# Mixture-of-experts layer: one region of rows per expert for the whole input instead of one per batch, and outputs put together block by block

## What is computed

```
x = x + attention(layernorm(x), ctx, ctx, mask) @ W_out.T
z = layernorm(x)
q = tanh(z @ proj_w.T / 0.3);  logits = -(6 - q @ anchors.T) / 2 / temp
top 2 of 6 experts, softmax of their logits -> expert_weights
h = gelu(z @ w1[e]);  x + sum over the 2 experts e of weight[e] * (h @ w2[e])
```

## Time and profile before

| | before |
|---|---|
| three runs, median (range) | 720.03 us (714.55 to 720.48) |
| the profiled execution | 721.91 us, its span in the trace 720.2 us |
| PE busy | 617.0 us (86%) |
| DVE busy | 451.5 us (63%) |
| ACT busy | 341.8 us (47%) |
| POOL busy | 301.0 us (42%) |
| moved by DMA | 126.25 MB, mean 175 GB/s |
| chain that ended last | PE 55%, DVE 14%, issue 11%, DMA 7%, POOL 5% |

### The profile page before, as it was taken

One profiled execution on the slowest core, in us unless ns is written; L12 is line 12 of the kernel. 1 busy time (PEld: TensorE's weight loads), 2 busy tenths in 40 slices (PEclk: granted clock), 3 DMA queues, 4 the chain that ended last, 5 costly groups with the idle time before them and its releaser, 6 DMA issues.

```text
span 720.2 us, 15169 instructions
## 1 busy us (share of the span) xinstructions
PE 617.0 (86%) x4628; PEld 467.8 (65%) x4629; DVE 451.5 (63%) x968; ACT 341.8 (47%) x646; POOL 301.0 (42%) x434
## 2 busy tenths in 40 slices
PE   5989999999999999988788999999999999996000
PEld 4765566666656656444568898998999888885000
DVE  4846756665685866444986555684555676666455
ACT  4536855666847655574844554433333333331000
POOL 5423755555456656557671314130002233222774
PEclk9759999999999999899987999999999999999555
DMA  5301213222212373347372656485787788886787
GB/s 187 93 30 46 88 63 101 76 87 75 88 59 101 108 271 129 133 172 263 132 263 88 208 174 239 149 273 203 263 293 244 256 268 285 295 277 220 226 246 243
DMA packets 62577, 126.25 MB, mean 175 GB/s; under 512 B 7974, under 2 KB 11046, under 8 KB 62508
## 3 DMA queue, kind: packets, MB, share of 16 engines
q1 hardware_dynamic: 52268, 91.80, 37.7%
q0 software_dynamic: 10240, 33.56, 14.5%
HBM read 69.24 MB, written 56.10 MB: 174 GB/s over the span
## 4 chain that ended last, share of the span: by engine, by line
PE 55%; DVE 14%; issue 11%; DMA 7%; POOL 5%; SPq 3%; ACT 2%; DVEq 1%; POOLq 0%; ACTq 0%
PE ps L1477 7%; DMA y_d<-ysb 5%; PE ps L1499 4%; PE ps L1635 4%; PE ps L1522 3%; PE ps L1687 3%; PE ps L1524 3%; PE ps L1688 3%; PE ps L1523 3%; PE ps L1689 3%; PE ps L1711 3%; PE ps L1713 3%; PE ps L1673 3%; PE ps L1712 3%; PE ps L1590 3%
## 5 line engine op out<-in xcount | busy, mean ns | idle before, releaser
L802 POOL DMA_INDIRECT yg<-y_d,sidx x64 | 64.1, 1002 | 170.4 <-DVE wst L1320 133.9
L1078 DVE TENSOR_REDUCE nmax<-ps 128x4 f32<-128x512 f32 x128 | 82.3, 686 | 45.6 <-PE ps L1477 45.4
L917 ACT ACTIVATE prob<-ps 128x512 f32<-128x512 f32 x128 | 66.1, 603 | 84.2 <-PE ps L1502 81.4
L729 POOL DMA_INDIRECT xs_d<-x,place_now x64 | 67.2, 1049 | 81.0 <-PE ps L1689 66.8
L1687 PE MATMUL ps<-w1H,xgH 128*128 x296 | 90.5, 306 | 2.9 <-DVE xgL L1344 2.9
L1688 PE MATMUL ps<-w1H,xgL 128*128 x296 | 83.9, 283 | 0.0
L1689 PE MATMUL ps<-w1L,xgH 128*128 x296 | 83.8, 283 | 0.0
L996 ACT ACTIVATE xgH<-ps 128x512 fp32r<-128x512 f32 x74 | 44.2, 597 | 80.9 <-PE ps L1673 68.7
L1477 PEld LDWEIGHTS ps<-kfT,qT 32*128 32x128 f32 x1024 | 69.6, 202 | 18.9 <-issue 16.3
L1477 PE MATMUL ps<-kfT,qT 32*128 32x128 f32 x1024 | 76.9, 295 | 1.9 <-DVE nmax L1078 1.4
L1357 DVE COPY ysb<-ps 128x512 f32<-128x512 f32 x74 | 51.0, 689 | 31.4 <-PE ps L1713 19.6
(11 more groups left out here) (195 smaller groups left out, 1373.2 us busy)
## 6 DMA issues: line engine op xcount, KB each, us to landing
xg<-xs_d SPq DMA_DIRECT2D x74, 256.0 KB
y_d<-ysb SPq DMA_DIRECT2D x74, 256.0 KB
xin<-in_x SPq DMA_DIRECT2D x32, 256.0 KB, 2.7
x<-in_x SPq DMA_DIRECT2D x32, 256.0 KB
x_d<-x SPq DMA_DIRECT2D x32, 256.0 KB
x2t<-x_d SPq DMA_DIRECT2D x16, 256.0 KB, 4.1
x2c<-x_d SPq DMA_DIRECT2D x16, 256.0 KB, 4.7
out_x<-x2c SPq DMA_DIRECT2D x16, 256.0 KB
```

Of the source, the lines that this page charges most:

```text
L729: nc.gpsimd.indirect_dma_start(xs_d, bass.IndirectOffsetOnAxis(ap=place_now[:, n % 2, k, t:t + 1], axis=0), x2[:, n % 4, t, :], None).then ...
L802: nc.gpsimd.indirect_dma_start(yg[:, k, z, :], None, y_d[b], bass.IndirectOffsetOnAxis(ap=sidx[:, k, z:z + 1], axis=0))\
L917: nc.scalar.activation(prob[v % 2][:, h, :], ps[:, B_SC + h, :], ACT.Exp, scale=scale).then_inc(exp_done, 1)
L1078: nc.vector.tensor_reduce(nmax[:, n % 2, :, g * hpg + h], ps[:, token_bank(v, h), :].rearrange("p (t k) -> p t k", t=4), axis=AX.X, op=ALU ...
```

## The change

1. **One region for each expert** over both batches: `region` is 4096 + 128 rows. Only 6 tiles can be part filled in all, so `tiles` is (8192 + 6 x 127) // 128 = 69.
2. **Two lists of tiles.** The first `T1` = 32 - 5 = 27 tiles are full tiles of what the first four blocks (`NB1`) left; the other `T2` = 42 are ordered by the block whose rows complete them. So the tiles that hold the rows of blocks 0 to n are among the first `TILES_OF[n]`: 37 for n up to 3, then 45, 53, 61, 69. The new functions are `full_tiles`, `first_list`, `tiles_of_classes`, `first_of_classes`, `list_of` and `rows_to_tiles`. A list comes out with one tile in a partition (`lst`); PE turns it into a row (`turn_list`) and DVE keeps it (`keep_list`). `turn_list` for the first list is in the last step but one of attention, for the second in slot 23. `rows_of_tokens` runs for one block in a slot, slots 24 to 31.
3. **The router's blocks come every 7 slots** instead of 8, and one of the four transposes of a block (`t == 2`) moves to the slot's end.
4. **Padding once**: `fill_up` is called once, in slot 21, instead of once for each batch.
5. **Puts**: put c belongs to slot 46 + 4c // 3 (three in four slots), for all 32 in turn. Its gathers are issued two slots earlier (POOL also waits there for `up_ready`), its store two slots later, and the residual of put c + 16 is loaded five slots later; the first 16 residuals are loaded in slots 28 to 43. 23 puts have a slot in the loop, 9 come behind it. There are six buffers for gathered rows (`RY`), 16 for residuals (`RX`). The gathers read their row numbers straight from `y_row`, and `stage` is gone.
6. **The copy to `ysb`** is ACT's from tile 26 (`BY_ACT`) on.
7. **Everything is written out**: 19 iterations, 76 slots, where there were 20 iterations and 80 slots with hardware loops in them.

The core of the diff:

```diff
-    NT = (2 * seq + EXPERTS * (P - 1)) // P
-    tiles = batches * NT
+    NB1 = blk_per_batch
+    region = batches * seq + P
+    def most_tiles(n):
+        return (2 * n * blk + EXPERTS * (P - 1)) // P
+    T1 = 2 * NB1 * blk // P - (EXPERTS - 1)
+    tiles = most_tiles(nblk)
+    TILES_OF = [most_tiles(max(n + 1, NB1)) for n in range(nblk)]
+    RY, RX, RD = 6, 16, 4
...
-        SPAN = 8
+        SPAN = 7
-        TABLE = SPAN * LATE - 1
+        TABLE = SPAN * (LATE - 1) + 5
...
+        ONE_Y, BY_ACT = 20, 26
+        def put_slot(c):
+            s = TILES_OF[0] + 9 + 4 * c // 3
+            return s if s < SLOTS and TILES_OF[c // 4] < tiles else None
...
+                    for c in puts(TPI * i + k - 2):
+                        store_out(c)
+                    for c in puts(TPI * i + k - 5):
+                        if c + RX < ntok:
+                            load_residual(c + RX)
...
+            def fetch_outputs(c):
+                pool.wait_ge(yrow_done, c // 4 + 1)
+                after(pool, cmb_done, c - RY + 1)
                 for z in range(2):
+                    nc.gpsimd.indirect_dma_start(yg[:, c % RY, z, :], None, y_d[0:TILES_OF[c // 4] * P, :],
...
+                    for c in puts(TPI * i + k + 2):
+                        pool.wait_ge(zp_ready, nblk)
+                        pool.wait_ge(up_ready, min(TPI * i + k - L_UP + 1, tiles))
+                        landed(c)
+                        fetch_outputs(c)
...
+                    w, p, n = tl(i, k, L_DN)
+                    if live(w, tiles) and w >= BY_ACT:
+                        act.wait_ge(y_ready, w + 1)
+                        after(act, y_out[p], 16 * n)
+                        nc.scalar.activation(ysb[:, p, :], ps[:, y_bank(w, p), :], ACT.Copy).then_inc(ya_done, 1)
...
+            def turn_list(bank, count):
+                pe.wait_ge(lst_done, count)
+                for z in range(2):
+                    last = nc.tensor.transpose(ps[0:1, bank, z * P:(z + 1) * P], lst[:, z:z + 1], ident[:])
+                last.then_inc(lst_turned, 1)
...
+            pe.wait_ge(tab_done, 2)
             for t in range(4):
                 project(INSIDE, t)
-            pe.wait_ge(tab_done, 3)
...
+                    if TPI * i + k == TABLE + 4:
+                        pe.wait_ge(used_done, nblk)
+                        turn_list(B_LATE, 2)
```

More of the change, by code:

```diff
@@ L80, in xattn_moe @@
     x2_d = dram("x2_d", [nblk, 4, P, emb], F32)
-    xs_d = dram("xs_d", [batches * rows, emb], F32)
+    xs_d = dram("xs_d", [rows, emb], F32)
     x2_rows = x2_d.rearrange("n t p d -> (n t) p d")
-    y_d = [dram(f"y{b}_d", [NT * P, emb], F32) for b in range(batches)]
+    y_d = dram("y_d", [tiles * P, emb], F32)
     ctx = ExitStack()
@@ L652, in _ @@
+            expert_loop(experts)
+            left = [c for c in range(ntok) if put_slot(c) is None or put_slot(c) + 2 >= SLOTS]
+            for c in left:
+                store_out(c)
+            for c in range(RD):
+                sp.wait_ge(o_out[c], 16 * (ntok // RD))
         @block.gpsimd
@@ L1292, in attention @@
                 if (i, q) == (blk_per_batch + 2, 0):
-                    tiles_of_experts(0)
+                    full_tiles()
                 if (i, q) == (blk_per_batch + 2, 1):
-                    experts_of_tiles(0)
-                if (i, q) == (blk_per_batch + 2, 2):
-                    rows_of_tiles(0)
-                    table(0)
+                    first_list()
                 if (i, q) == (blk_per_batch + 2, 3):
-                    rows_of_tokens(0)
+                    keep_list(B_SC, 0, T1)
                 setup(s)
@@ L1353, in experts @@
                     w, p, n = tl(i, k, L_DN)
-                    if live(w, tiles):
+                    if live(w, tiles) and w < BY_ACT:
                         dve.wait_ge(y_ready, w + 1)
@@ new lines, in experts @@
+                    if TPI * i + k == TABLE + 2:
+                        first_of_classes()
+                    if TPI * i + k == TABLE + 3:
+                        list_of(CLASSES, nblk)
+                        dve.wait_ge(share_done, nblk)
+                    if TPI * i + k == TABLE + 4:
+                        keep_list(B_LATE, T1, T2)
+                        rows_to_tiles()
+                    rows_of_tokens(TPI * i + k - TABLE - 5)
+                    for c in puts(TPI * i + k):
+                        put_together(c)
@@ L1403, in _ @@
+            expert_loop(experts)
+            for c in range(ntok):
+                if put_slot(c) is None:
+                    put_together(c)
         @block.tensor
```

516 lines of the change are left out of this document (238 added, 278 removed).

## The result

The changed kernel takes 676.98 us (median of four runs, 674.82 to 682.66); the kernel before, on the same chip, 719.83 us (714.55 to 720.48). The ratio is 0.943, with a 95% interval of 0.936 to 0.949. The forecast was 687, with a range of 670 to 708. Direction and range held; the kernel came out 10 us faster than the number.

A forecast was written before the change was run, and what follows sets the result against it. PE was taken to bound the loop, with transfers sharing from slot 50, then a tail of POOL's gathers. 567.3 (slot 50's copy) + 68 (dense) + 20.4 (last six slots) + 31.3 (tail) = 687.0 us; range 670 to 708.

The forecast's parts named there:

- PE's pace to slot 50: Expert loop up to slot 50: a slot is PE's work, 3.47 us each.
- signs of being wrong: Wrong if slots 51 to 67 stay at 3.5 us or pass 4.7, or the loop before slot 50 loses over 6.
- the first rival: Slots 51 to 67 stay at PE's pace, 59 us, with a tail of 27.7: 672 us in all; chance 0.17.
- The tail: Behind the last copy: 22 gathers issued one by one by POOL, 1.42 us apart, 31.3 us instead of 56.8.
- The dense slots: Slots 51 to 67: 83 transfers, 21.8 MB, paced by the DMA engines, 68 us, 4.0 a slot.
- a full share is 331 to 336 GB/s: DMA ceiling for slots 51 to 67, from 288 GB/s at share 0.87 and 272 at 0.81.
- The last six slots: Six slots from slot 67 to the last copy in slot 73: 20.4 us, as the last six took before.
- The list: Head of slot 23: PE waits 3.4 us for the second list, plus 2.0 us for the lower clock.
- The router's 8.8 us: Slots 5 to 20: the router's work is the same, so its 8.8 us stay, in 7 slots a block.
- The padding: Moves from slots 32 and 33 to slot 21 at equal price.
- The end of attention: Ahead of the expert loop: the list `used` comes 1.8 us earlier but PE waits for `keep_list`, net +0.6 us.

The follow-up runs named there:

- again2: The changed kernel, unchanged, repeated a second time: 678.46 us, 0.943 of the kernel before.
- half_puts: Changed kernel with put c at slot 46 + 2c, so 15 puts in the loop and 17 behind it: 696.72 us, 0.970.
- full_puts: Changed kernel with one put in every slot from slot 46 on, 28 in the loop and 4 behind it: 680.81 us, 0.942.
- extra1: Changed kernel with one extra 256 KB store of zeros in each of slots 51 to 67: 686.82 us.
- again: The changed kernel, unchanged, repeated for a second profile: 678.57 us, 0.945 of the kernel before.
- spread_fill: Changed kernel with the six padding transfers issued one per slot in slots 20 to 25, not all in slot 21: 678.92 us.
- extra2: Changed kernel with two extra 262,144-byte stores of zeros in each of slots 51 to 67: 702.54 us.
- fill_late: Changed kernel with all six padding transfers issued in slot 24 instead of slot 21: 690.62 us.
- late_turn: Changed kernel with the second list's transposes moved from the head to the end of PE's slot 23: 679.73 us, 0.943.
- before_again: The kernel before, unchanged, profiled a second time; slot 5's copy came at 395.26 us, whole time not given.

## Why the prediction was right, and where its sum was off

The direction was right, for the reason given: five tiles fewer and a shorter tail. Along the columns of the table, from before to `again2`: -1.9, +2.7, +6.7, -4.5, -19.9 and -25.7 us, -42.6 in sum. The last two are the five slots fewer and the tail, the two losses the router and slots 22 and 23, and the dense slots gained 4.5 us with more transfers in them. PE's pace to slot 50 and a tail of gathers were foreseen rightly; that the dense slots would be the DMA engines' was wrong. Two of the prediction's own signs of being wrong came: slots 51 to 67 stayed at 3.5 us, and the loop up to slot 50 lost more than 6 us (8.5 in the first profile, 9.4 in `again2`, from slot 5 on). The range held because its lower part had been left open for the first rival.

*The tail.* Forecast 31.3, measured 31.3, 31.2 and 31.1. Its parts are nearly as forecast: the first of 22 gathers 6.3 us ahead of the last copy (7.7 in the sum), 1.36 us apart (28.58 / 21; 1.42 in the sum), the data 5.0 us behind the last. Two small misses cancel.

*The dense slots: the step that was off by 8 us.* The forecast was 68 us, 4.0 a slot; it is 59 to 60, 3.46 to 3.56 a slot, which is PE's pace. The step that failed is the division of a rate by a share: "both say that a full share is 331 to 336 GB/s". At a share of 0.87 before there were 288 GB/s, and 300 at 0.91 in `half_puts`; but 368 at 1.02 in the kernel after and 392 at 1.04 in `full_puts`. From 0.91 to 1.04 the share grows by 14% and the rate by 31%. A packet's time, of which the share is made, isn't a fixed price: a gather's packets of 3.3 kB took 194 ns on average in the stretch of the second row, 149 in the dense slots after and 138 in `full_puts`, at the higher rate; SP's packets of 1.8 kB took 87 ns in the stretch of the first row, 79 and 77 in the other two. Why they get shorter is not shown. Read from `full_puts` and `extra1`, the sum would have had 21.8 MB at 392 GB/s, 55.5 us, under PE's 59.

The trace of the kernel before could have said so. "The trace has never held more than 288 GB/s" is true of stretches of 31 us, in which bunches of transfers and gaps are averaged. Windows of 3 and 2 us, inside the stretches of the two rows:

```profile
533.00:536.00 3.00, 3.00 (x24) 2.78 (x23) 1.42 (x3) 1.21 (x3) 0.00 (x0) 1.00 1.03 380
616.00:618.00 2.00, 2.00 (x14) 1.73 (x13) 0.80 (x2) 0.61 (x3) 0.00 (x0) 1.00 1.05 389
```

At a share over 1 the kernel before moved 380 and 389 GB/s, not 334. These are the highest windows of their length there, and such short ones flatter: in `full_puts` slices of 1.7 us reach 415 where the mean is 392. But even at 360 the 21.8 MB need 60 us, about PE's 59, and not 68.

The Trainium skill points the same way: "Perfetto Trace Analysis", Identifying the Most-Contended Engine, wants transfers judged by their bandwidth and not by occupancy, which sixteen engines make misleading. By the runs here that is right. And the ceiling of 392 GB/s lies between the two figures cited in the prediction, above the 358 of one core's share. The same page of the Trainium skill, under Roofline, has a single active core pull more than that share, up to about 435; 392 is within that.

So the first rival's mechanism is what happened, and not the forecast's. That rival had a chance of 0.17 and a time of 672; the two repeats came out 5 to 6 us above that. Its tail of 27.7 us (gathers 1.25 apart) didn't come, which is 3.4 us by `again2`; the router is 2.7, slots 20 to 50 are 1.3 and the last six slots 0.8; and 2.5 us ahead of slot 5 go the other way.

*The last six slots.* Forecast 20.4, measured 17.7 to 18.8; the rival's 18 was nearer. Two of the six intervals of before held waits of the kind in the earlier trace rows, 1.4 and 2.6 us.

*The list.* Forecast a wait of 3.4 us and 2.0 for the lower clock. The window of slots 22 to 23 has 8.74 us with 5.66 of PE: 3.1 of waiting, and 2.2 more of PE's work than a slot's 3.47, at a mean clock of 0.61. That is 5.3 against 5.4. In `again` and `again2` the same slot takes 9.51 and 9.46 us, so the list costs 5.3 to 6.0. PE's own wait is 5.26 us only because the lateness of slot 22 is in it.

*Slot 22.* Not foreseen: 5.61 us instead of 3.47, 2.1 us, and 5.5 to 5.7 in ten of the twelve profiles (6.7 in `spread_fill`, 7.3 in `extra2`). PE's records of that slot are complete and end at 459.2, as they should, but ACT, DVE and POOL receive its signals about 2.8 us late. It is not the padding (`spread_fill`, `fill_late`), not the place of the list's turn (`late_turn`, 3.54 us of wait in the same row) and not the low clock, which in `late_turn` begins only at 473.2, behind it. Four scatters of the last block are issued back to back there, from 454.56 on, at a share near 1; no run moved them. Against them speaks that the two blocks ahead have four back to back too (from 396.42 and 426.67 on), with no signal that late behind them, and that in `fill_late` the share is 0.63 and 0.70 from 461 to 465, while its slot 22 is as late. The cause stays open.

*The router's 8.8 us.* Forecast to stay; the seven slots of a block cost 2.6 us more. The failed step is "The router's work is the same": the work is, but the order isn't, and the change said so in its third point. In the order of the changed kernel transpose 2 stands directly ahead of transpose 3 in one bank, and that could be read before any run.

*The padding.* Forecast at an equal price; it costs nothing to be seen at slot 21, where before it made 1.4 us (5.69 + 2.60 us in slots 33 and 34, less 6.9; 1.0 in `before_again`). Slots 20 to 50 come out right by this: 105.4 - 1.4 + 5.3 + 2.1 = 111.4 for the first profile, measured 111.3; 112.1 in the repeats with their 6.0. The forecast's 110.8 had neither slot 22 nor the padding's gain: two misses of 2.1 and 1.4 us that happen to cancel in part.

*The end of attention* cannot be told: +0.6 is lost in the 10 us by which executions differ ahead of slot 5. In `late_turn` and `fill_late`, whose lower clock falls at the places of before's up to 336 us, slot 5 comes 0.4 to 0.7 us behind before's two profiles. That leaves room for the +0.6, but 0.3 of it is there already at 203 us.

All in all, `again2` (677.6) against the forecast: -2.5 ahead of slot 5, +2.7, +1.3, -9.1, -1.6 and -0.2 along the columns of the table, -9.4 in sum. The largest term is the dense part, which was thought to be the DMA engines'. That the whole is off by no more than that one term is luck: the others add up to -0.3.

## What to carry to other kernels

Don't scale a DMA rate by its busy share to find the ceiling; take a measured rate at a share over 1.0. Look for it in windows of 2 or 3 us: a mean over 30 us holds the gaps between bunches as well (288 GB/s there, where 3 us of it have 380). If the trace has none, keep the highest rate of any row as a lower bound of what is possible. Transfers can be moved from a tail into a loop for almost nothing until bytes per slot over the slot's time reach the ceiling (here 392 GB/s); past it the tail's gain is paid in the loop (9.9 us gained and 8.3 lost in `full_puts`). When two small transposes share a bank, an edit that changes their spacing can have a price even though no work was added (2.6 us here).

## What the runs showed of the hardware that was not expected

- One core moved 386 to 392 GB/s for 67 to 80 us (device memory to and from the core's buffers, gathers included), at a share of 1.02 to 1.04.
- Padding of six transfers of 262,144 bytes, issued together, cost nothing to be seen in slot 21, just ahead of PE's wait for the list, 1.0 to 1.4 us in slots 33 and 34 of the kernel before, and 6 us in slot 24 (`fill_late`, with a stretch of lower clock).
- The start of the expert loop varied over 10 us (388.9 to 399.4) between executions whose attention code is the same, in good part with the places at which PE's lower clock was granted. Such a difference must not be put down to a change: of the 14 us between forecast and first profile, 3 to 4 were of this kind.
- In one slot the signals of PE reached ACT, DVE and POOL about 2.8 us behind its recorded work, in ten of twelve profiles, and otherwise late in the other two, unexplained.
- The same packets took less time at a higher rate: a gather's 194 ns at 272 GB/s, 149 at 368, 138 at 392.
